# All experts' W1 in one load, copied to a slot on VectorE, with a new order of the work

## The reference, cut to what matters

```
x1 = x + attention0(norm(x)) + ffn0(norm(x))       # norm: layer norm without weights
x2 = x1 + attention1(norm(x1)) + ffn1(norm(x1))
attention0: 16 heads, weight of a key 1 + s/4 + (s/4)^2/2 = ((1 + s/4)^2 + 1)/2 for s = q.k, causal, divided by their sum
ffn0:       8 experts of 64 (all computed, weighted by a top-2 choice) and a shared one of 128
attention1: q.k of the same token only, a softmax over the batch, times the sum of v over the tokens
ffn1:       e = argmax(softmax(xn @ w_red @ wg_n.T))       # one of 8 experts for each token
            out = score * (gelu(xn @ w1[e] + b1[e]) @ w2[e] + b2[e])      # w1[e]: 128 x 512, w2[e]: 512 x 128
```

## Time and profile before

| | us |
|---|---|
| median of 3 runs | 267.4 (266.67 to 270.66) |
| profiled execution | 267.27 |
| its span, first to last instruction | 265.5 |
| TensorE busy | 252.0 (95%) |
| VectorE busy | 178.7 (67%) |
| ScalarE busy | 145.2 (55%) |
| GpSimd busy | 80.2 (30%) |
| mean granted clock of TensorE | 0.980 |
| W1 loads by SyncE | 23 of 256 KB, 3.7 us from issue to landing (median of 16) |

### The profile page before, as it was taken

How to read it: one execution, slowest core, us unless ns; L and a number is a source line. 1 busy time by engine, 2 the same in 40 slices (tenths; PEclk the granted TensorE clock), 3 DMA queues, 4 the chain that set the end, 5 groups by cost and what they waited for, 6 DMA issues and landing times.

```text
span 265.5 us, 6541 instructions
## 1 busy us (share of the span) xinstructions
PE 252.0 (95%) x2215; PEld 167.4 (63%) x2215; DVE 178.7 (67%) x497; ACT 145.2 (55%) x262; POOL 80.2 (30%) x116
## 2 busy tenths in 40 slices
PE   6799999999999999999999999999999899999980
PEld 5454653345566545457646765655988778999870
DVE  4788748888855288954588698897778926323340
...
GB/s 137 233 257 139 4 209 182 154 257 208 159 206 147 2 1 2 0 2 0 2 0 2 13 11 23 20 79 87 148 4 40 110 186 245 227 152 219 182 22 0
DMA packets 40335, 27.05 MB, mean 102 GB/s; under 512 B 5104, under 2 KB 35872, under 8 KB 40304
## 3 DMA queue, kind: packets, MB, share of 16 engines
...
q0 software_dynamic: 3264, 2.12, 4.3%
...
## 4 chain that ended last, share of the span: by engine, by line
PE 79%; issue 6%; DVE 5%; POOL 4%; DMA 3%; POOLq 1%; SPq 0%; ACT 0%; DVEq 0%; ACTq 0%
PE SC L904 15%; PE YT L924 14%; PE WB L876 14%; PE WB L964 7%; PE WB L862 5%; POOL out_dram L673 3%; PE SC L827 3%; PE WB L944 3%; PE WB L953 2%; PE WB L888 2%; PE YT L837 2%; PE WB L869 1%; PE SC L837 1%; DMA y_dram<-KT,ROW 1%; PE WB L942 1%
## 5 line engine op out<-in xcount | busy, mean ns | idle before, releaser
L739 ACT ACTIVATE A<-SC 128x2048 f32<-128x2048 f32 x40 | 75.2, 1879 | 42.8 <-PE SC L904 37.5
L539 POOL TENSOR_TENSOR RSTD<-VE,NHALF 128x2 f32<-128x2 f32 (+1 forms) x13 | 11.1, 851 | 136.0 <-DVE VE L1068 136.0
L904 PE MATMUL SC<-QM,KT 32*128 32x512 f32 (+1 forms) x384 | 46.8, 557 | 0.3 <-DVE QM L1387 0.3
L1295 DVE SCALAR_TENSOR_TENSOR A<-A,TRI 128x1024 f32<-128x1024 f32 x32 | 38.5, 1227 | 3.9 <-ACT A L739 3.9
L924 PE MATMUL YT<-A,VH 128*18 128x256 f32 (+1 forms) x768 | 40.1, 345 | 0.0
L673 POOL DMA_INDIRECT out_dram<-KT,ROW x18 | 28.0, 1553 | 19.6 <-DVE KT L1305 15.8
L924 PEld LDWEIGHTS YT<-A,VH 128*18 128x18 f32 x768 | 20.4, 97 | 20.8 <-issue 5.4
L699 ACT ACTIVATE QM<-SC,B1T 128x128 f32<-128x128 f32 x72 | 20.5, 368 | 12.2 <-PE SC L827 11.6
L904 PEld LDWEIGHTS SC<-QM,KT 32*128 32x128 f32 x384 | 17.1, 183 | 14.0 <-issue 11.0
L620 POOL DMA_INDIRECT xs_dram<-XN,POS x16 | 16.4, 1026 | 15.9 <-DVE POS L1177 11.7
L876 PE MATMUL WB<-XNT,WU 128*128 128x512 f32 x40 | 20.7, 607 | 0.0
...
## 6 DMA issues: line engine op xcount, KB each, us to landing
...
W1S<-in_L_ffn_w_dram SPq DMA_DIRECT2D x16, 256.0 KB, 3.7
HT<-in_L_ffn_w_dram SPq DMA_DIRECT2D x7, 256.0 KB
...
out_dram<-X SPq DMA_DIRECT2D x4, 256.0 KB, 3.5
X<-_attn_hidden_states_dram SPq DMA_DIRECT2D x3, 256.0 KB, 3.8
HT<-y_dram SPq DMA_DIRECT2D x3, 256.0 KB, 3.1
```

What stands on the lines that cost most here:

```text
L739: act.activation(squares(n).rearrange("p k r c w -> p r k (c w)"), SC[:, :, 0:k * w].rearrange("p r (k w) -> p r k w", k=k), ACT.Square, b ...
L904: last = pe.matmul(SC[:, r, cols].rearrange("p (c w) -> p c w", w=width), KT[rows, b % 2, blk, i * P:(i + 1) * P], QM[rows, b % 2, blk, 0: ...
L1295: dve.scalar_tensor_tensor(out=a, in0=a, scalar=1.0, in1=keep, op0=ALU.add, op1=ALU.mult).then_inc(masked, 1)
```

## The change

A new region name `W1R` stands for the first two of the three places of `A`, 128 x 4096 numbers, as many as all eight experts' W1 have. When the last of the 40 `av` products is done (`av_done`), SyncE loads all of `w1` there in one DMA of 2 MB. The five early slots keep their own loads. For a late slot k a new function `copy_w1` on VectorE waits until the place in `W1S` is free, loads the slot's expert into a register and copies 128 x 512 numbers from `W1R`; TensorE's `up` waits for that copy. The first three copies are items of their own (`wc`), each later one stands at the head of `fi`, three slots ahead. In SyncE's loop only the loads of x are left. The whole list `PLAN` is in a new order; it has the same items and three more (`wc.0` to `wc.2`). The diff shows its end and the place with the least work between two score groups.

```diff
--- before.py
+++ after.py
@@ -56,6 +56,7 @@
 SUMS_AT = 3
 SAVE_AT = 5
 IDS_AHEAD = 3
+W1_AHEAD = 3
 PLANNED = 6
 RT_STEPS = 8
 
@@ -105,50 +106,50 @@
...
-s.34 sx.1 av.32 xd.3 ra.1 x2.4 g.17 pd.3 sq.35
-s.35 rs.5 av.33 av.34 l2.5 x2.5 es.1 xd.4 pd.4 rk.1 xd.5 ra.2 sx.2 g.18 sq.36 pd.5 es.2 sx.3 sq.37
-s.36 u.17 rk.2 sx.4
-s.37 n.6 av.35 w.14 sx.5 mk.37
-s.38 sq.38 mk.38 av.36 g.19 u.18 sx.6 tk.0 ew.0 u.19 w.15 mk.39
-s.39 av.37 sq.39 av.38 sx.7 at.6 et.0 of.6 sx.8 ys.39 av.39 et.1 oa.6 eu.0 n.7 sx.9 sx.10 sx.11 rs.6 l2.6 of.7 at.7 x2.6
-et.2 oa.7 eu.1 xd.6 pd.6 rs.7 ed.0 l2.7 ra.3 es.3 ey.0 ed.1 x2.7 rk.3 sx.12 et.3 hc.0 xd.7 ra.4 eu.2 eu.3 pd.7 es.4 ey.1
-rk.4 ed.2 sx.13 et.4 eu.4 sx.14 hc.1 sx.15 ed.3 ed.4 hp.0 vb.0 tx.0 pt.0 pt.1 hp.1 tx.1 up.0 up.1 pa.0 pt.2 sm.0 pt.3
-sm.1 pa.1 vb.1 tx.2 pa.2 sm.2 pa.3 tx.3 dn.0 fi.0 up.2 dn.1 tx.4 up.3 dn.2 tx.5 fi.1 ey.2 up.4 dn.3 tx.6 fi.2 ey.3 fi.3
-up.5 ey.4 dn.4 fi.4
...
+s.22 sq.22 wt.2 av.20 k.6 mk.21
+s.23 sq.23 at.2 sq.24 mk.22 q.6 n.3 rs.1
...
+s.34 ys.32 av.31 sq.34 av.32 sx.2 x2.4 xd.3 g.17 ra.1
+s.35 av.33 sq.35 av.34 rs.5 l2.5 pd.3 es.1 x2.5 rk.1 sq.36 u.17 xd.4
+s.36 pd.4 sx.3 xd.5 sx.4 ra.2 g.18 pd.5 g.19
+s.37 es.2 rk.2 u.18 sq.37 mk.37 w.14
+s.38 sx.5 vp.3 sx.6 mk.38 av.35 av.36 sx.7 n.6 sq.38 sx.8 sx.9 ew.0 u.19 w.15 sq.39 sx.10 mk.39
+s.39 av.37 av.38 at.6 of.6 et.0 sx.11 av.39 ys.39 oa.6 eu.0 tk.0 rs.6 n.7 l2.6 of.7 at.7 x2.6 et.1 oa.7 et.2 rs.7 xd.6
+pd.6 eu.1 l2.7 ed.0 hc.0 x2.7 ra.3 es.3 ed.1 xd.7 pd.7 et.3 rk.3 ra.4 eu.2 ey.0 et.4 es.4 ey.1 rk.4 ed.2 eu.3 vb.0 hp.0
+eu.4 ed.3 hc.1 vb.1 ed.4 wc.0 hp.1 wc.1 tx.0 tx.1 sx.12 wc.2 up.0 pt.0 pt.1 up.1 fi.0 dn.0 pa.0 pa.1 sm.0 sm.1 pt.2
+sx.13 pt.3 sm.2 tx.2 pa.2 pa.3 sx.14 fi.1 tx.3 up.2 sx.15 tx.4 ey.2 ey.3 fi.2 dn.1 up.3 dn.2 up.4 fi.3 tx.5 dn.3 tx.6
+fi.4 ey.4 dn.4 up.5
@@ -293,6 +294,7 @@
         YO = [KT[:, n // 8, n // 4 % 2, n % 4 * D:(n % 4 + 1) * D] for n in range(Y_SLOTS)]
         W1S = [sb(f"W1S{n}", [P, F1]) for n in range(W1_SLOTS - W1_SPARE)]
         W1S = W1S + [HT[:, 0, EARLY_B + n] for n in range(W1_SPARE)]
+        W1R = A[:, 0:2].rearrange("p s r l -> p (s r l)")
         YE = [HT[:, 0, b] for b in range(EARLY_B)]
         XTS = [sb(f"XTS{n}", [P, P]) for n in range(2)]
         GE = [QM[:, 0, n, 0] for n in range(2)]
@@ -361,6 +363,8 @@
         ids_kept = sem("ids_kept")
         early_done = sem("early_done")
         out_saved = sem("out_saved")
+        w1_resident = sem("w1_resident")
+        w1_copied = sem("w1_copied")
         w1_loaded = [sem(f"w1_loaded{n}") for n in range(W1_SLOTS)]
         xs_loaded = [sem(f"xs_loaded{n}") for n in range(U)]
         x_turned = sem("x_turned")
@@ -463,12 +467,8 @@
             sp.dma_start(rows, INIT[:, 0:D].rearrange("p (o d) -> p o d", o=1).to_broadcast([P, NT, D])).then_inc(y_cleared, 16)
 
             def load_w1(s, e):
-                w = s - W1_SLOTS
-                if 0 <= w < EARLY:
-                    wait_made(sp, ("eu", w))
-                at_least(sp, up_done, w - EARLY + 1)
                 src = w1[bass.ds(e, 1)].rearrange("o d f -> d (o f)")
-                sp.dma_start(W1S[s % W1_SLOTS][:], src).then_inc(w1_loaded[s % W1_SLOTS], 16)
+                sp.dma_start(W1S[s][:], src).then_inc(w1_loaded[s], 16)
 
             def load_slot(s, row):
                 if U <= s < U + EARLY:
@@ -500,19 +500,13 @@
                 if s == 0:
                     sp.wait_ge(early_scattered, 16 * EARLY_TILES)
                 load_slot(s, both // E1)
+            sp.wait_ge(av_done, len(groups()))
+            sp.dma_start(W1R.rearrange("p (e f) -> p e f", e=E1), w1.rearrange("e d f -> d e f")).then_inc(w1_resident, 16)
             sp.wait_ge(slots_ready, 1)
-            first = []
-            for k in range(FIRST):
-                both = slot_word(SLOT, k)
-                load_w1(EARLY + k, both % E1)
-                first.append(both // E1)
+            rows = [slot_word(SLOT, k) // E1 for k in range(FIRST)]
             sp.wait_ge(xs_scattered, 16 * (NT - EARLY_TILES))
-            for k in range(FIRST):
-                load_slot(EARLY + k, first[k])
-            for k in range(FIRST, LATE):
-                both = slot_word(SLOT, k)
-                load_slot(EARLY + k, both // E1)
-                load_w1(EARLY + k, both % E1)
+            for k in range(LATE):
+                load_slot(EARLY + k, rows[k] if k < FIRST else slot_word(SLOT, k) // E1)
                 if k == SUMS_AT:
                     for s in range(EARLY):
                         sp.wait_ge(y_saved[s], 16)
@@ -821,7 +815,7 @@
             def up(n):
                 s = EARLY + n
                 pe.wait_ge(xt_copied, n + 1)
-                pe.wait_ge(w1_loaded[s % W1_SLOTS], 16 * (s // W1_SLOTS + 1))
+                pe.wait_ge(w1_copied, n + 1)
                 at_least(pe, gelu_done, n - 1)
                 for k in range(NF):
                     last = pe.matmul(UP[n % 2][:, k * P:(k + 1) * P], W1S[s % W1_SLOTS][:, k * P:(k + 1) * P],
@@ -995,7 +989,7 @@
                     last = pe.transpose(w[:, 0:P], XSL[n][:, 0:D], IDF[:])
                 if kind == "eu":
                     wait_used(pe, ("et", n))
-                    pe.wait_ge(w1_loaded[n % W1_SLOTS], 16 * (n // W1_SLOTS + 1))
+                    pe.wait_ge(w1_loaded[n], 16)
                     for k in range(NF):
                         last = pe.matmul(w[:, k * P:(k + 1) * P], W1S[n % W1_SLOTS][:, k * P:(k + 1) * P],
                                          XTS[n % 2][:], start=(k == 0), stop=True, skip_group_check=True)
@@ -1314,10 +1308,25 @@
                 dve.wait_ge(y_summed, n + 1)
                 score(s)
 
+            def copy_w1(k):
+
+                s = EARLY + k
+                w = s - W1_SLOTS
+                if k == 0:
+                    dve.wait_ge(slots_ready, 2)
+                    dve.wait_ge(w1_resident, 16)
+                if 0 <= w < EARLY:
+                    wait_made(dve, ("eu", w))
+                at_least(dve, up_done, w - EARLY + 1)
+                e = dve.value_load(SEXP[0:1, k:k + 1], min_val=0, max_val=E1 - 1)
+                dve.tensor_copy(W1S[s % W1_SLOTS][:], W1R[:, bass.ds(e * F1, F1)]).then_inc(w1_copied, 1)
+
             def late_slot(n):
 
                 for k in range(0 if n == 0 else n + IDS_AHEAD, min(n + IDS_AHEAD + 1, LATE)):
                     keep_ids(EARLY + k)
+                if n + W1_AHEAD < LATE:
+                    copy_w1(n + W1_AHEAD)
                 finish(n)
 
             for kind, n in plan:
@@ -1397,6 +1406,8 @@
                     add_sums(n)
                 if kind == "pa":
                     add_heads(n)
+                if kind == "wc":
+                    copy_w1(n)
                 if kind == "fi":
                     late_slot(n)
                 if kind == "et":
```

More of the change, by code:

```diff
@@ L107 @@
 ls.0 ln.0 ls.1 xt.0 ln.1 qa.0 ka.0 xt.1
-s.0 ls.2 q.0 g.0 ls.3 g.1 k.0 k.1 v.0 ln.2 v.1 ln.3 xt.2 u.0 g.2 k.2 vp.0 sq.0 ls.4 u.1 q.1 u.2 g.3 mk.0
-s.1 sq.1 u.3 ln.4 q.2 g.4 xt.3
-s.2 sq.2 av.0 xt.4 v.2 v.3
-s.3 v.4 mk.1 mk.2 v.5 u.4 ys.2 sq.3 v.6 v.7 lg.0 av.1 av.2
-s.4 rt.0 g.5 rt.1 u.5 sq.4 g.6 n.0
-s.5 av.3 sq.5 av.4 rt.2 g.7
-s.6 av.5 rt.3 cn.0 sq.6 rt.4 u.6 g.8 rt.5 rt.6
-s.7 at.0 sq.7 u.7 sq.8 mk.7 q.3 k.3
-s.8 av.6 av.7 rt.7 mk.8 u.8
-s.9 sq.9 oa.0 g.9 g.10 mk.9
-s.10 wt.0 av.8 av.9 w.0 sq.10 w.1
@@ L119 @@
-s.11 k.4 ys.9 sq.11 mk.10 q.4 n.1 mk.11 u.9 w.2 sq.12 mk.12
-s.12 av.10 g.11 q.5
-s.13 w.3 av.11 sq.13 av.12 wt.1
-s.14 sq.14 ys.12 at.1 of.0 w.4 sq.15
-s.15 av.13 sq.16 vp.1 av.14 cw.0
-s.16 n.2 of.1
-s.17 av.15 av.16 oa.1
-s.18 u.10 sq.17 u.11 mk.17 cm.0 sq.18 sq.19
-s.19 at.2 k.5 av.17 mk.18 mk.19 w.5
-s.20 w.6 rs.0 sq.20 wt.2 av.18 av.19 w.7 ys.19
-s.21 q.6 q.7 sq.21 g.12 mk.20
-s.22 mk.21 l2.0 oa.2 sq.22 g.13 sq.23 u.12
-s.23 av.20 mk.22 av.21 x2.0 sq.24 u.13 rs.1 g.14
-s.24 ys.22 av.22 l2.1 n.3 av.23 sq.25 w.8
@@ L151 @@
-up.5 ey.4 dn.4 fi.4
+s.0 sq.0 ls.2 q.0 k.0 q.1 g.0 g.1 ln.2 u.0 ls.3 k.1 g.2 xt.2 v.0 sq.1 ls.4 mk.0
+s.1 ln.3 g.3 u.1 v.1 av.0
+s.2 xt.3 sq.2 mk.1 u.2 ln.4 u.3 g.4 sq.3 v.2
+s.3 v.3 v.4 mk.2 av.1 av.2 xt.4 v.5 q.2 v.6 v.7 vp.0 sq.4
+s.4 u.4 g.5 u.5
+s.5 lg.0 ys.2 sq.5 g.6 g.7 rt.0 rt.1 sq.6 q.3 rt.2
+s.6 av.3 vp.1 sq.7 rt.3 av.4 rt.4 av.5 u.6
+s.7 n.0 u.7 rt.5 rt.6 k.2
+s.8 sq.8 mk.7 av.6 g.8 u.8 k.3 mk.8 sq.9 rt.7
+s.9 g.9 g.10 mk.9 u.9
+s.10 sq.10 av.7 cn.0 wt.0 av.8 g.11 sq.11 mk.10 w.0
+s.11 w.1 w.2 av.9 k.4 ys.9 w.3 mk.11
@@ new lines @@
+s.12 sq.12 mk.12 sq.13 av.10 of.0 sq.14
+s.13 wt.1 av.11 sq.15 av.12 w.4 w.5
+s.14 of.1 w.6
+s.15 at.0 k.5 av.13 ys.12 av.14
+s.16 sq.16 u.10 g.12 oa.0 u.11 w.7 vp.2
+s.17 cw.0 av.15 av.16 sq.17 sq.18
+s.18 mk.17 rs.0 u.12 mk.18 g.13 sq.19 q.4
+s.19 q.5 mk.19 l2.0 n.1
+s.20 ys.19 av.17 sq.20 av.18 av.19 x2.0 u.13 mk.20
+s.21 at.1 sq.21 of.2 oa.1 n.2
+s.22 sq.22 wt.2 av.20 k.6 mk.21
+s.23 sq.23 at.2 sq.24 mk.22 q.6 n.3 rs.1
+s.24 ys.22 av.21 l2.1 av.22 k.7 of.3 x2.1 g.14 cm.0 sq.25
+s.25 w.8 av.23 at.3 sq.26 u.14 n.4 oa.2
@@ new lines @@
```

(11 more changed lines are left out.)

9 lines of the change are left out of this document (removed).

## The result

The changed kernel takes **275.12 us** (median of 3 runs, 274.24 to 275.15) where the kernel before took 267.4: 1.0256 times the time, 95% interval 1.0148 to 1.0364. The forecast was 267.6 us within 265.2 to 270.4. The profiled executions are 275.15 (span 273.4) and 267.27 us (span 265.5): 7.9 us to find.

A forecast was written before the change was run, and what follows sets the result against it. Bound: a full TensorE wall from 10 to 193 us, then GpSimd's 18 late scatters, started once X's stores land. Terms -0.5 + 0.1 + 0.4 + 0.3 = +0.3 on 267.27 gave 267.6 us, range 265.2 to 270.4.

The forecast's parts named there:

- no hole, price 0: Between two score groups: TensorE's least other work, about 2.1 us, covers ScalarE's 1.88 us square, so the new order costs 0.
- +0.3, bounds 0 and 1.0: From `oa.7` to VectorE's last addition to X: the new order makes that addition end at 224.5 against 224.24 us.
- 1.7 us are added on TensorE, of which 0.7 reach the last addition: If the clock falls again at about 206.9 us: 1.7 us more on TensorE, 0.7 at VectorE's last addition to X.
- TensorE's own slots get shorter at places: price 0: Late slots: the new order shortens some TensorE slots, but GpSimd ends the kernel, so 0 unless VectorE paces the tail.
- Copies, port, traffic: Late slots and stores of X: lighter traffic -0.5 us, VectorE's copies +0.1, waits between copies and scatters at the port +0.4.
- The load: hidden: The 2 MB W1 load, issued at about 191 us, lands at about 201, first wanted at 211: price 0.
- The order tears the wall: Rival, 10 to 193 us: a ring bank or first early X 1 us over its cover; 2 to 7 us, 6%.
- wrong if TensorE idles in the middle: Sign against the forecast: it expected no gap of TensorE between 10 and 193 us.
- Scatters first at 227.9 to 229.3: Sign for the forecast: the first of GpSimd's 18 late scatters starts at 227.9 to 229.3 us.

The follow-up runs named there:

- group four: Runs on chip 3 against the kernel before (267.82 us): changed kernel again 1.0249, old order with copies 1.0027, two mixes of the orders cut at `ed.4` 1.0071 and 1.0283.
- old_order_copies_again: The kernel before, its order kept, with the one large W1 load and VectorE's copies, on chip 3: 268.81 us, 1.0027 of the kernel before.

## Why the prediction was wrong

**The order up to `oa.7`: "no hole, price 0".** This step failed first. I compared TensorE's work between two score groups with ScalarE's 1.88 us. "I followed each engine's list", I wrote, but of GpSimd's I looked only at the part behind 190 us, and missed that `rs.0` had got a neighbour. The step also took equal busy time for equal progress. With the new front the wall is full, 182.97 of 183 us, and `oa.7` comes 1.9 us later all the same. Sized at 0, it is 1.8; on chip 1 the new front without the hole costs 1.0085, 2.3 us (1.1 to 3.5).

**Behind `oa.7`: "+0.3, bounds 0 and 1.0".** The term that was mis-sized most. The gap ahead of `rk.4` was foretold with 1.2 us, and 0.99 came; the kernel before idles as long, 0.32 us ahead of `rk.4` and 0.68 ahead of `eu.4`. But of the half clock I wrote that 1.7 us are added on TensorE, of which 0.7 reach the last addition: I had taken its length from the trace of before, 3.4 us, where it lasts up to 10.2, and had let VectorE's sums hide what was over. They hide nothing of it: section C is 1.0 us longer than before, not shorter. Some 0.6 of that were in the sum (0.9 for `dn.0` less 0.3 for `vb.1`). B costs 4.1 us in the first pair of traces, of which up to 2.7 are the long half clock of that execution, and, by the two ranges, 0.4 to 5.5.

**"TensorE's own slots get shorter at places: price 0".** Failed. D is 1.1 us longer, of which the order before with copies has 0.5, and in group four the order behind `ed.4` costs 1.2 us more than the copies. The scatters' step is 1.85 to 1.9 as foretold; the new order adds waits between them.

**Copies, port, traffic.** Right in mechanism and nearly in size. VectorE's slot is 1.89 for 1.97, and 0.7 us (0 to 1.4) were measured for -0.5 + 0.1 + 0.4. The gain of 0.5 from lighter traffic came, but not to the end. In old_order_copies_again the last store of X lands 2.47 us after its issue and not 3.53, at 227.36 where it was 227.85 before. VectorE's first late result then comes at 227.85 where it was 226.76, so GpSimd now waits for VectorE and starts at 228.71 against 228.64; the scatters take 32.82 us from first to last against 31.78. The port costs less per meeting than the 0.4 that I took as the most: in the trace after, six scatters with a copy beside them take 1.60 to 1.62 us, the seven others with one 1.53 to 1.57, as do most without. The copy's 0.43 us is near my lower bound of 0.39, as the Trainium skill, VectorE: DVE Perf Modes, section "Mode 2×_2P — use both read ports for one tensor", has it. What the Trainium skill, GPSIMD Engine Reference, section "8. Key points", says of instructions with two SBUF inputs is borne out on the other side as well: GpSimd's two additions took 1.47 and 1.33 us beside the masks and 0.46 to 0.55 elsewhere in that trace.

**The load: hidden.** Right; it was complete at 204.4, later than the 202 that I gave, and first used at 214.4.

**The rivals.** "The order tears the wall", 269 to 275 us at 6%, gave 2 to 7 us; measured are 6.6 to 7.7. That its number nearly fits is luck: its condition was a bank of the ring or the first early X coming late, the hole that did tear is worth 0.7 us, and more is lost behind the wall than in it. A rival for the order as a whole deserved far more than 6%: a whole list of some four hundred items was rewritten, and I had priced two places of it. Of my signs, "wrong if TensorE idles in the middle" was the one that fell due. "Scatters first at 227.9 to 229.3" failed by 5.5 us.

**What I could not have foreseen from one trace** is the stop. The kernel before takes 267.4 to 269.4 us on three occasions and 275.3 to 276.3 on three others, chips 6, 7 and 13; the changed one 274.4 to 275.1 on all three where it was timed. Where the stop is, "no difference", the forecast's verdict, is what is measured, for a reason that it didn't have. Each chip was used in one session, so the stop may belong to the chip or to the session.
